# Four-layer graph kernel on one core: pruning by stored byte marks, a seventh buffer for the next pass, a reordered node softmax and a rebuilt last normalisation

## What is computed

```python
att = softmax((Q @ (H.T @ V).T) * scale * H, axis=1)           # passes edge, att
comp_mask = softmax(0.5*structural + 0.5*att.mean(0)) >= th
cos = xn @ xn.T                                                # pass cos
edge_mask = (softmax(cos * H, axis=1) >= th_edge) & comp_mask[:, None]
H_pruned = H * edge_mask
connectivity = H_pruned.sum(axis=1)
node_mask = (softmax(connectivity * feat_mag) >= th_node) & (connectivity > 0)
vdeg = maximum(H_pruned.sum(axis=1), 1e-6); edeg = maximum(H_pruned.sum(axis=0), 1e-6)
agg = (H_pruned.T * vdeg**-0.5) @ ((x_comp * node_mask) @ W) / edeg   # pass down
x = relu((vdeg**-0.5 * (H_pruned @ agg)) @ Theta)                     # pass up
...
out = layernorm(x_in + x)      # (v - mean) / sqrt(var + 1e-5)
```

## Time and profile before

| | |
|---|---|
| median of 3 runs | 1704.54 us (1704.5 to 1704.84) |
| the profiled execution's own time | 1703.35 us |
| its span in the trace | 1701.5 us |
| granted TensorE clock, mean | 0.979 |
| PE / DVE / ACT / POOL busy | 87% / 68% / 42% / 22% of the span |
| moved by DMA | 578 MB, 340 GB/s over the span |

### The profile page before, as it was taken

One profiled execution on the slowest core, in us unless ns is written; L12 is line 12 of the kernel. 1 busy time (PEld: TensorE's weight loads), 2 busy tenths in 40 slices (PEclk: granted clock), 3 DMA queues, 4 the chain that ended last, 5 costly groups with the idle time before them and its releaser, 6 DMA issues. The chain is left out here.

```text
span 1701.5 us, 24198 instructions
## 1 busy us (share of the span) xinstructions
PE 1472.3 (87%) x10145; PEld 633.4 (37%) x10171; DVE 1150.8 (68%) x1623; ACT 721.4 (42%) x636; POOL 366.2 (22%) x255
## 2 busy tenths in 40 slices
PE   6789998999999998777787799998997777787895
PEld 2234433434344343333332344443443333332442
DVE  0000213677613997999989798126998999988897
ACT  0000101533211775999910233014776999700441
POOL 0000000000000894644400000003985444200000
PEclk9999999999999999899999999999999999999998
DMA  9979597899799995566589999999993666599993
GB/s 401 426 296 407 221 425 316 276 329 408 300 423 382 427 422 225 206 241 244 197 346 427 422 419 427 426 426 422 412 408 129 232 242 235 201 425 425 427 425 151
DMA packets 60620, 578.41 MB, mean 340 GB/s; under 512 B 6240, under 2 KB 6496, under 8 KB 20832
## 3 DMA queue, kind: packets, MB, share of 16 engines
q1 hardware_dynamic: 60512, 576.87, 84.0%
HBM read 575.14 MB, written 1.70 MB: 339 GB/s over the span
## 5 line engine op out<-in xcount | busy, mean ns | idle before, releaser
L1432 DVE CUSTOM_DVE_ANT_1 pairs<-ps,slot 128x832 f32<-128x832 f32 x352 | 342.4, 1022 | 15.5 <-issue 8.2
L633 PE MATMUL ps<-slot,cur 128*64 128x512 f32 (+1 forms) x1536 | 281.8, 516 | 33.7 <-DVE slot L1614 19.3
L1162 ACT ACTIVATE pairs<-pairs,negmax 128x3327 f32<-128x3327 f32 x88 | 269.9, 3067 | 75.2 <-DVE negmax L1443 75.2
L633 PE MATMUL ps<-hats 64*128 64x416 f32 x832 | 182.3, 557 | 93.2 <-DVE max L1432 92.6
L574 POOL TENSOR_SCALAR cur<-pairs,row_rz 128x768 f32<-128x768 f32 x32 | 70.5, 2204 | 874.0 <-DVE row_rz L1534 869.2
L633 PE MATMUL ps<-arena 64*128 64x416 f32 (+1 forms) x1072 | 208.2, 525 | 1.0 <-DMA arena<-adj 0.4
L633 PEld LDWEIGHTS ps<-slot,cur 128*64 128x64 f32 x1536 | 103.6, 137 | 207.9 <-issue 163.8
L1585 DVE SCALAR_TENSOR_TENSOR slot<-pairs,cut,slot 128x2687 f32<-128x2687 f32 (+1 forms) x52 | 161.4, 3105 | 0.1
L1178 ACT ACTIVATE arena<-pairs,cut 128x3328 fp8e4<-128x3328 f32 x52 | 159.0, 3058 | 2.6 <-DVE cut L1576 1.8
L633 PEld LDWEIGHTS ps<-hats 64*128 64x128 f32 x832 | 73.7, 193 | 176.8 <-DVE max L1432 136.8
L1208 ACT ACTIVATE hats<-ps 128x2048 int16<-128x2048 int16 (+1 forms) x28 | 42.1, 1554 | 225.7 <-PE ps L985 225.6
(11 more groups left out here) (198 smaller groups left out, 1826.9 us busy)
## 6 DMA issues: line engine op xcount, KB each, us to landing
slot<-adj SPq DMA_DIRECT2D x162, 1664.0 KB, 9.7
slot<-adj_t SPq DMA_DIRECT2D x64, 1664.0 KB, 15.7
arena<-adj_t SPq DMA_DIRECT2D x26, 1664.0 KB, 23.8
arena<-adj_t SPq DMA_DIRECT2D x52, 832.0 KB, 6.8
arena<-adj SPq DMA_DIRECT2D x15, 1664.0 KB, 14.6
pairs<-adj SPq DMA_DIRECT2D x15, 1664.0 KB, 15.6
pairs<-adj_t SPq DMA_DIRECT2D x12, 1664.0 KB, 14.1
hats<-adj SPq DMA_DIRECT2D x8, 1664.0 KB, 14.7
```

The source lines that it names most:

```text
L633: return pe.matmul(o, l, r, start=start, stop=stop, skip_group_check=True)
L1162: act.activation(bufs[b][:, 0:N], bufs[b][:, 0:N], ACT.Exp, bias=negmax[:, b:b + 1], accum_out=rowsum[:, b:b + 1]).then_inc(exp_done, 1)
L1432: dve.tensor_tensor_reduce(out=pieces3(bufs[k % len(bufs)], c), in0=pieces_psum(piece_place(name, k, c)[0]), in1=pieces3(slot_of(name, k), ...
```

## The change

1. **Byte pruning.** `prune` of block k below 24 reads ACT's sign bytes instead of the f32 product. It waits for `product_free` (ACT's sign of block k) instead of `row_cut`. The first piece of a block no longer waits for `pruned`. The split of the columns is now by halves: DVE has 2 x 1376, POOL and ACT's sum 2 x 288, the padding column included, which POOL's new `memset` sets in the product.
2. **Seventh home.** Home 8 is `shared[NP:2*NP]`, over `hat_right` and the first half of `prod[0]`. It serves down for k below 20; the first streamed blocks of down go to homes 4, 8 and 5.
3. **Node softmax behind cosine.** ACT takes the degree's root before the exponential; DVE forms 1/root and the scaled threshold while it waits, and one instruction replaces three behind the sum.
4. **Last block of up.** DVE prunes it in two pieces, 2 x 1024 and 2 x 640 columns; PE starts behind the first.
5. **The end.** x is scaled by the degree's root in the middle of up 1 (2 DVE instructions), and epsilon by its square, so that one instruction makes ReLU plus x; ACT centres, squares and sums part 0 block by block, and writes parts 0 and 1. `centre_part` has two instructions instead of three.

```diff
-LATE_SLOTS = 8
+LATE_SLOTS = 9
+DOWN_HOMES = (4, 8, 5)
+HELD = 20
-SHARE = 640
+SHARE = 288
+OWN = HALF - SHARE
...
+                if kind == "down" and k < HELD:
+                    homes = DOWN_HOMES[k - KEPT_BLOCKS:][:1] or (*homes, 8)
...
+                    if kind == "down" and home == 8 and k < 7:
+                        sp.wait_ge(piece_read, (2 * it + 2) * NB * 4 + 5)
+                        sp.wait_ge(pruned, it * PRUNES + NB - 1)
+                        sp.wait_ge(product_free, (2 * it + 2) * NB + 1)
...
             def cut_of(it, k):
+                pool.wait_ge(piece_read, ((2 * it + 1) * NB + k) * 4 + 4 + 5)
+                pool.memset(prod[k % 2][:, N:NP], -HUGE)
                 pool.wait_ge(exp_done, (2 * it + 1) * NB + k + 1)
...
+                root(small["structural"][:, :], small["edeg"][:, :], deg_sq, it + 1, deg_rt)
                 node_exp(2 * it + 1)
-                root(small["dv"][:, :], small["edeg"][:, :], deg_sq, it + 1, deg_rt)
...
                 if it == 1:
-                    for c in range(3):
-                        square_part(EARLY_LNS + 3 + c, c)
-                        root_part(EARLY_LNS + 3 + c, c)
+                    act.wait_ge(end_mean, 1)
+                    for b in blocks_of(0):
+                        act.activation(scr_b[:, b * D:(b + 1) * D], scr_a[:, b * D:(b + 1) * D], ACT.Square,
+                                       bias=small["imp"][:, b:b + 1], accum_out=small["conn"][:, b:b + 1])\
+                            .then_inc(end_squares, 1)
+                    square_part(EARLY_LNS + 3, 1)
+                    end_root(0)
+                    act.wait_ge(end_bias, 1)
+                    for b in blocks_of(0):
+                        act.activation(cur[:, b * D:(b + 1) * D], scr_a[:, b * D:(b + 1) * D], ACT.Identity,
+                                       bias=small["imp"][:, b:b + 1], scale=small["var"][:, b:b + 1]).then_inc(out_ready, 1)
+                    end_root(1)
+                    square_part(EARLY_LNS + 4, 2)
...
                         dve.wait_ge(product_free, g * NB + k + 1)
                         if k >= 2:
-                            dve.wait_ge(pruned, g // 2 * PRUNES + k - 1)
                             dve.wait_ge(share_marked, g // 2 * SHARED + min(k - 1, SHARED))
...
+                    if k < SHARED:
+                        dve.wait_ge(product_free, (2 * it + 1) * NB + k + 3)
+                        own = halves(slot[:, :])[:, :, 0:OWN]
+                        marks = interleaved(signs[:, row * NP:(row + 1) * NP])[:, :, 0:OWN]
+                        dve.scalar_tensor_tensor(out=own, in0=marks, scalar=0.0, in1=own, op0=ALU.is_le, op1=ALU.mult,
+                                                 accum_out=conn).then_inc(pruned, 1)
...
-                link(above(S["imp"], th_node))
-                link(dve.tensor_tensor(S["imp"], S["imp"], S["colsum"], ALU.mult))
-                dve.wait_ge(deg_rt, it + 1)
-                link(dve.reciprocal(S["dv"], S["dv"]))
-                link(dve.tensor_tensor(S["imp"], S["imp"], S["dv"], ALU.mult))
+                link(dve.scalar_tensor_tensor(out=S["imp"], in0=S["imp"], scalar=tiny["gsum"][:, 0:1], in1=S["colsum"],
+                                              op0=ALU.is_ge, op1=ALU.mult))
...
+                    if it == 1 and k == NB // 2:
+                        dve.wait_ge(kept, 32)
+                        dve.scalar_tensor_tensor(out=S["rnorm"], in0=S["structural"], scalar=LN_EPS, in1=S["structural"],
+                                                 op0=ALU.mult, op1=ALU.mult)
+                        link(dve.tensor_tensor(blocks3(xw[:, :]), blocks3(xw[:, :]), per_node(S["structural"]), ALU.mult))
...
+                link(dve.scalar_tensor_tensor(out=of_part(scr_a, c), in0=part_psum(c), scalar=0.0, in1=of_part(xw[:, :], c),
+                                              op0=ALU.max, op1=ALU.add))
+                link(dve.tensor_reduce(mean, of_part(scr_a, c), axis=X, op=ALU.add))
```

More of the change, by code:

```diff
@@ L171, in late_places @@
             else:
-                slot = min(HOMES[kind], key=lambda s: last[s])
+                homes = HOMES[kind]
+                if kind == "down" and k < HELD:
+                    homes = DOWN_HOMES[k - KEPT_BLOCKS:][:1] or (*homes, 8)
+                slot = min(homes, key=lambda s: last[s])
                 free = last[slot] + 1
@@ L590, in prune_share @@
             def prune_share(it, k):
-                slot = slot_of(f"cos{it}", k)
-                cols = slice(N - SHARE, N)
+                product, slot = (halves(t)[:, :, OWN:HALF] for t in (prod[k % 2], slot_of(f"cos{it}", k)[:, :]))
+                marks = halves(share_marks[:, :])
                 pool.wait_ge(row_cut, it * NB + k + 1)
```

123 lines of the change are left out of this document (88 added, 35 removed).

## The result

| | before | after |
|---|---|---|
| median of 3 runs | 1704.54 us | 1691.67 us (1691.28 to 1692.13) |
| ratio after / before | | 0.9927, 95% interval 0.9912 to 0.9942 |
| profiled execution / its span | 1703.35 / 1701.5 us | 1691.28 / 1689.3 us |
| granted clock, mean | 0.979 | 0.980 |

The change gains 12.9 us; I had forecast 16.6 us and 1687.9 us. The median lies inside the range, 3.8 us above the forecast. To see where the 3.8 us are I cut both traces at the same instructions.

What follows compares the result with a forecast made beforehand. Loads bound the long stretches, DVE with ACT right behind bounds cos. Terms 4.0 + 8.0 + 1.7 + 0.4 + 1.0 + 1.5 = 16.6 us off 1703.35 give 1686.7; the median 1.2 higher, 1687.9 us; range 1681.0 to 1697.0.

Steps and rivals of the forecast that it cites:

- Cos: Cos passes: byte pruning shortens the block period from 7.21 to 7.06 us, gaining 2.0 us a pass, 4.0 in two.
- The first prune's 2.78 us wait: First block of each cos pass: the prune waits 2.78 us for ACT's sign, net -2.3 us a pass.
- Rival 3: Cos: POOL's two instructions over split column runs become a third slower and hold DVE, costing 30 us: 1718; chance 0.05.
- Rival 1: Cos: the piece keeps its 0.22 us idle, 10.2 us less gain: 1698.1 us; chance 0.1.
- Down: Start of down: a seventh home lets loads get one block ahead, 3.99 us an iteration, 8.0 together.
- Rival 2: Down: the seventh home saves nothing because DVE or PE bounds down once loads are ahead: 1695.9 us; chance 0.1.
- Node softmax: Seam of cos and down: `cur` starts 0.85 us sooner, 1.7 us in two, counting in full.
- Last block of up: Up's last block, pruned in two pieces: PE starts 0.95 us sooner and never waits, gaining 1.0 us.
- The end: From the end's first DVE instruction to its last: 13.5 us instead of 15.05, gaining 1.5 us.
- Earlier layers: `centre_part` in the earlier layers loses one small DVE instruction of 0.2 us; behind decay two parts gain 0.4 us.

Runs made afterwards that it cites:

- e1_code: The changed kernel with one more tiny POOL elementwise instruction right behind the all-reduce that precedes cos, in both iterations; 1684.72 us.
- e2_dvememset: The changed kernel with a product's one-column pad set by DVE ahead of the block's maximum, and POOL's memset with its wait removed; 1683.02 us.
- e8_first: e1_code with the first block of each cos pass pruned from the float product instead of sign bytes; 1680.73 us.
- e4_pruned: The changed kernel with the old wait of a block's first piece for the prune just ahead of it put back; 1704.33 us.
- e5_sixhomes: The changed kernel with home 8 not used by down; 1698.08 us.
- e9_fill: The changed kernel with eight filler matmuls on PE ahead of the column sums of cos's last block but one; 1688.20 us.
- b1: The changed kernel with the edits of e1_code and e8_first, twelve fillers before the last column sums, the root's table loaded beside up 1, a reordered end; 1681.79 us.

## Why the prediction came out as it did

The total is near in part by luck. Two errors of 6 to 7 us in cos stand against each other; with the period as forecast and the memset as it is the median would have been about 6 us higher, 1697.7 us (an estimate from the trace), just outside my range.

- **Cos: 3.5 us gained, 4.0 forecast, by two wrong terms.** "The period becomes 7.21 - 0.22 + 0.07 = 7.06 us" failed low: it is 6.93, since the wait cost 0.30 us and not the visible 0.22, and the 65 more columns 0.01 us and not 0.07. Over 23 periods that is 3.0 us a pass more than forecast. "POOL's memset of one column falls in POOL's idle time ahead of the threshold and costs nothing" failed high: with it ahead of the `cut`, the first prune waits 6.1 and 6.3 us instead of 2.78, 3.3 to 3.5 us a pass; e1_code and e2_dvememset, which put a cheap instruction ahead of it or take it away, gave back 7.0 and 8.7 us, of which the two cos passes hold 6.4 and 6.7. The memset was bounded from above by "another POOL instruction of one column", a row of an instruction in the middle of a stream. The row that I should have asked was the first POOL instruction behind the reduction, which had 10.48 us between it and the reduction and so could hide 7 us.
- **The first prune's 2.78 us wait is real, 2.72 and 2.99 us in e1_code**, and it can't simply be had back: the f32 prune runs into POOL (e8_first).
- **POOL meeting DVE.** The earlier trace rows showed DVE's prune at 3.84 us instead of 3.01. In the changed kernel the 48 byte prunes have a mean of 3.02 us, so none is held up by a multiply. Rival 3 did not come: POOL's two instructions take 1.72 and 1.28 us, no longer than before. Its ground holds, as e8_first shows with 4.58 us for POOL's 1.72. That is the rule of the Trainium skill's page "SBUF — State Buffer" (section "SBUF: two separate sides"), which the trace bears out from both sides: here POOL is the one that waits.
- **Rival 1** (the piece keeps its gap) did not come, but e4_pruned shows its price: 12.7 us by the medians, where I had 10.2.
- **Down: right.** Forecast 8.0 us in two iterations; e5_sixhomes puts it at 7.8 by the stretches of the trace. Rival 2 fell: DVE ran at its own pace for long stretches and still met the stream before the end of down.
- **Node softmax: mechanism right, worth less, and not passed on.** `cur` comes 0.67 us sooner instead of 0.85, because `conn` to `cur` takes 3.48 and not 3.3 us. "It counts in full, since PE's gathers behind it free the homes" failed: PE's own column sums and keep-busy matmuls came last at the lower clock, and the seam lost 1.0 us in two instead of gaining 1.7. Where the clock was up, the seam is 7.01 us, a gain of 0.68. PE's rows were absent from my working of this place. Root and exponential stand 0.02 us behind their table loads again. The Trainium skill (page "ScalarE: Activation LUTs", section "What ACT_TABLE_LOAD costs") adds a drain of 1.38 us to each; no load of this trace shows one.
- **Last block of up: 0.5 us, forecast 1.0.** From its prune's start to the copy out of PSUM 6.24 us (1665.12 to 1671.36) instead of 6.75. The gathers of the two blocks before took 7.50 us at a lower clock, so PE came late; in e9_fill, where they took 3.02 and 3.01 us, the whole stretch of the end is 20.94 instead of 21.61 us, and the split is worth about 1.2.
- **The end: right,** 1.5 us, with squares at 0.33 us (0.34 forecast) and scalings at 0.33 with both pointers and 0.23 with one (0.28 forecast). The sum hid two errors: the scalings of part 0, with two pointers, took 2.76 us and those of part 1, with one, 2.00 (2.2 forecast for each), and the table load (1678.16 to 1679.44) cost next to nothing, because DVE reached the variance of part 0 only at 1679.39.
- **Earlier layers: not shown.** att 0 starts 0.23 us sooner (545.13 to 544.90; 0.4 forecast), but it starts anywhere from 544.35 to 545.72 us in the profiles of the new kernels, which do not differ up to there, so the profiles can't tell 0.4 us. Ahead of cos 0's first piece 0.42 or 0.43 us of "issue" stands in all twelve new profiles, where before it was 0.07: this 0.36 us is an effect of the change, and I found no cause.
- **Edge 1's 0.6 us** was not in the sum. The stretch is 109.64 to 110.48 us over all thirteen profiles, none of which differs there from the changed kernel but the one of before, so I take it for spread and no effect of the change.

Against the 16.6 us, the seams are short by 2.7 us (1.7 forecast, -1.0 come), cos by 0.5, the last block of up by 0.5, the earlier layers by 0.5, edge 1 by 0.6 that was not in the sum; down and up have 0.3 more than forecast. That is 4.5 us, and 16.6 - 4.5 = 12.1 us, the distance of the two profiled executions (1703.35 to 1691.28). The medians are 12.9 us apart.

## What to carry to other kernels

Before you call an instruction free because its engine is idle there, ask whether it is the first of its kind behind another kind of work, and what the trace's gaps could be hiding. A wait on one's own engine's last instruction costs its visible gap and the overlap that it forbids, here 0.22 + 0.08 us a block; to put it back in 48 blocks cost 12.7 us by the medians. At a seam, price every engine that comes last, also the one whose clock may be down, since what one chain gains there another can keep.

## What the runs showed of the hardware

- POOL takes about 7 us from a PARTITION_ALL_REDUCE to its first TENSOR_SCALAR (6.98 to 7.20 us in the six passes of e1_code, e8_first and b1, and 6.75 to 7.83 us in twelve passes in which a memset stands between, counted from the memset). The time passes under that instruction's own wait (e2_dvememset), but not under the wait of the memset ahead of it. The Trainium skill (page "GPSIMD Engine Reference", section "2.1 Instruction dispatch") says that the first call of freshly loaded code pays about 6 us without an instruction in the profile. That would fit the reduction and the elementwise instructions needing different code, with a gap 1 us longer than its figure; no run here shows what is loaded.
- TensorE's granted clock differs from seam to seam of the same program: column sums of 28 matmuls take from 1.71 to 3.20 us. Eight matmuls in the idle time ahead of them hold it up: 1.71 us in 4 seams of 4, against 0 of 22 without. Where PE's work is the same, the distance from `conn` to the next loads goes with it, from 7.0 us to 8.2.
- A POOL comparison that starts 0.04 us behind a DVE prune with two f32 inputs takes 4.58 us instead of 1.72.
- A wait of DVE for its own last instruction costs 0.30 us a block: 3.25 us from the start of a prune to the start of the piece behind it in e4_pruned, 2.94 us in the changed kernel.
- On ACT, instructions of 64 columns follow each other every 0.33 us with a bias and a scale pointer, or with a bias pointer and a sum, and every 0.23 us with one pointer.
